# A one-block vision transformer on one core: ternary weights turned through low bf16 halves, score bias by row groups, warm-up from a constant tensor, value factors and scale row apart

## What is computed

```python
h = patches @ W.T + b + pos_emb                       # 512 x 256
z = layernorm(h)
k, q, v = split(z @ W_kqv + b_kqv)                    # 16 heads of 16
a = softmax(q @ k.T / 4 + slopes * tril(j - i), causal)
h = h + (a @ v) @ W_proj + b_proj
z = layernorm(h)

def bitlinear(x, w):
    scale = clip(mean(abs(w), axis=1), 1e-5)
    tern = clip(round(w / scale), -1, 1)
    return x @ (tern * scale).T
r = relu(bitlinear(z, w_fc) + gate * (z @ v.T @ fast_b.T @ u.T))   # 1024 hidden
out = h + bitlinear(r * r, w_proj)
```

## Time and profile before

| | before |
|---|---|
| median of 3 runs | 71.55 us (71.11 to 71.77) |
| the profiled execution | 70.84 us |
| its span in the trace | 69.0 us |
| PE busy in the span | 61.9 us (90%) |
| weight loads (PEld) | 55.6 us (80%) |
| DVE, ACT, POOL busy | 45.6, 38.4, 25.9 us |
| read from and written to memory | 6.08 and 0.52 MB |

### The profile page before, as it was taken

How to read it: one execution, slowest core, us unless ns; L and a number is a source line. 1 busy time by engine, 2 the same in 40 slices (tenths; PEclk the granted TensorE clock), 3 DMA queues, 4 the chain that set the end, 5 groups by cost and what they waited for, 6 DMA issues and landing times.

```text
span 69.0 us, 2144 instructions
## 1 busy us (share of the span) xinstructions
PE 61.9 (90%) x886; PEld 55.6 (80%) x886; DVE 45.6 (66%) x99; ACT 38.4 (56%) x76; POOL 25.9 (37%) x41
## 2 busy tenths in 40 slices
PE   3999999999989999999999967999976999999900
PEld 2787888889979999897988836989936899999900
DVE  1000029567999877997999783426596999969670
ACT  5200001824395969947779996737949338964000
POOL 6400408597779389999915000000000000000610
PEclk9999999999999999999999999999999999999997
DMA  0899999999810000000000000000000000000053
GB/s 0 269 310 312 321 385 410 419 362 369 311 64 0 9 0 0 0 9 0 9 0 0 9 5 5 0 0 9 0 0 0 0 0 0 0 0 0 9 176 128
DMA packets 3497, 6.74 MB, mean 98 GB/s; under 512 B 400, under 2 KB 1312, under 8 KB 3488
## 3 DMA queue, kind: packets, MB, share of 16 engines
q1 hardware_dynamic: 3488, 6.60, 26.5%
HBM read 6.08 MB, written 0.52 MB: 96 GB/s over the span
## 4 chain that ended last, share of the span: by engine, by line
PE 69%; DVE 12%; ACT 12%; issue 3%
PE psum L304 13%; PE psum L489 11%; PE psum L460 8%; PE psum L370 5%; PE psum L499 5%; PE psum L324 4%; PE psum L344 4%; PE psum L427 3%; PE psum L399 2%; DVE z L779 2%; PE psum L388 2%; PE psum L469 2%; ACT L696 2%; ACT fc_t L614 2%; PE psum L437 2%
## 5 line engine op out<-in xcount | busy, mean ns | idle before, releaser
L1043 POOL TENSOR_TENSOR tail_sb<-tail_sb,h 128x256 f32<-128x256 f32 x2 | 1.4, 732 | 26.3 <-DVE tail_sb L878 26.3
L719 ACT ACTIVATE head_sb<-psum,fc_scale 128x256 f32<-128x256 f32 x16 | 6.7, 470 | 4.6 <-PE psum L469 3.7
L593 ACT ACTIVATE std<-mv,eps_sb 128x1 f32<-128x1 f32 x8 | 2.2, 288 | 12.5 <-DVE mv L773 12.5
L489 PE MATMUL psum<-mlp_t,sq_hi 128*128 128x256 f32 x32 | 7.9, 285 | 1.1 <-DVE sq_lo L797 1.0
L489 PE MATMUL psum<-mlp_t,sq_lo 128*128 128x256 f32 x32 | 7.7, 281 | 0.0
L769 DVE TENSOR_TENSOR h<-psum,pos_sb 128x256 f32<-128x256 f32 x4 | 1.6, 412 | 8.9 <-PE psum L304 8.9
L489 PEld LDWEIGHTS psum<-mlp_t,sq_hi 128*128 128x128 f32 x32 | 6.0, 189 | 1.5 <-issue 1.5
L460 PE MATMUL psum<-zt_hi,fc_t 128*128 128x256 f32 x32 | 6.7, 281 | 0.0
L304 PE MATMUL psum<-head_sb 128*128 128x256 f32 x24 | 6.7, 445 | 0.0
L460 PE MATMUL psum<-zt_lo,fc_t 128*128 128x256 f32 x32 | 6.6, 278 | 0.0
L304 PEld LDWEIGHTS psum<-head_sb 128*128 128x128 f32 x24 | 5.5, 235 | 1.0
(11 more groups left out here) (111 smaller groups left out, 164.7 us busy)
## 6 DMA issues: line engine op xcount, KB each, us to landing
head_sb<-head SPq DMA_DIRECT2D x6, 256.0 KB, 4.2
fc_sb<-w_fc SPq DMA_DIRECT2D x2, 512.0 KB, 7.0
mlp_sb<-w_mlp SPq DMA_DIRECT2D x2, 512.0 KB, 8.9
tail_sb<-tail SPq DMA_DIRECT2D x2, 384.0 KB, 6.1
out<-tail_sb SPq DMA_DIRECT2D x4, 128.0 KB, 1.7
pos_sb<-pos SPq DMA_DIRECT2D x1, 256.0 KB, 4.6
kqv_sb<-w_k SPq DMA_DIRECT2D x1, 256.0 KB, 6.5
kqv_sb<-w_q SPq DMA_DIRECT2D x1, 256.0 KB, 6.7
```

The lines of the kernel that those rows point to most:

```text
L489: mm = pe.matmul(mlp_ps[f * BH + b], part[:, n % RING, a, b * P:(b + 1) * P], mlp_t[:, 2 * j + a, :], start=j == 0 and a == 0 and i == 0 a ...
L719: nc.scalar.activation(relu[:, n % PART_RING, a, :], FCB[n][:, a * HT:(a + 1) * HT], ACT.Relu, scale=fc_scale[:, 0, m:m + 1]).then_inc(rel ...
```

## The change

Four things are edited.

1. **Turning the ternary weights.** `ROUND` gets 2^14 added. The low 16 bits of the rounded float32 are then 0x4000 plus the whole number, and read as bf16 that is 2.0 for zero, a little more for a positive and a little less for a negative number. `fc_low` and `mlp_low` are views of these low halves (bf16, every second one). PE turns them as ordinary bf16 matmuls against `ident_bf`, and ACT subtracts 2 instead of `ROUND` before the sign. POOL has to make `ident_bf` from `ident`.
2. **Score bias.** The table has 128 columns instead of 256. Partitions 0 to 63 hold the heads of the first score bank, 64 to 127 those of the second; inside each 64, 32 rows are the high part and 32 the low part. `score_bias` is two matmuls with 64 rows each, against `select_r`, that adds a high and a low row. POOL makes `select_r` and subtracts twice on 32 partitions. The constants carry 8 columns more.
3. **Warm-up.** The 14 matmuls read a constant tensor of ones that exists before the program's first barrier, so `warm`, its memset on DVE and PE's wait for it go.
4. **Side products apart.** `fold_v` stays where `fold_v_spread_scale` was, without its wait for `mlp_scaled`. `spread_scale` stands behind `turn(0)` of the second layernorm, ahead of `turn_mlp(1)`. ACT's copy is 32 columns at the old place (`vf_sb`), and 256 columns (`scale_row`) behind `mlp_signs(1)`.

The core of the diff:

```diff
-ROUND = 1.5 * 2.0 ** 23
+ROUND = 1.5 * 2.0 ** 23 + 2.0 ** 14
...
-        warm = sb("warm", [P, HT], BF16)
+        ones = nc.const_aps.tensor(1.0, [P, HT], BF16)
...
+        fc_low, mlp_low = (w[:, :, :].rearrange("p m e -> p (m e)").bitcast(BF16).rearrange("p (w two) -> p w two", two=2)[
+            :, :, 0].rearrange("p (m e) -> p m e", e=n) for w, n in ((fc_whole, E), (mlp_whole, HID)))
...
             def score_bias(f):
-                pe.wait_ge(alibi_step, 4)
-                pe.wait_ge(identr_done, 1)
+                pe.wait_ge(alibi_step, 5)
+                pe.wait_ge(select_done, 1)
                 for r in range(2):
-                    for i, part in enumerate((alibi_hi, alibi_lo)):
-                        bias = part[:, r * HPG:(r + 1) * HPG, :].rearrange("p (o h) s -> p o (h s)", o=1)
-                        pe.matmul(s_ps[f][:, r, :], ident_r[:, :], bias.broadcast_to([P, BH, HPG * S]),
-                                  start=i == 0, stop=False, skip_group_check=True)
+                    rows = slice(r * 64, (r + 1) * 64)
+                    bias = bias_t[rows, :, :].rearrange("p (o h) s -> p o (h s)", o=1)
+                    pe.matmul(s_ps[f][:, r, :], select_r[rows, :, :].rearrange("p h s -> p (h s)"),
+                              bias.broadcast_to([64, BH, HPG * S]), start=True, stop=False, skip_group_check=True)
...
-            def fold_v_spread_scale():
+            def fold_v():
                 pe.wait_ge(v0_in, 16)
+                for k in range(KE):
+                    mm = pe.matmul(vf_ps[:, k * RANK:(k + 1) * RANK], v_sb[:, k * P:(k + 1) * P], v_sb[:, E:E + RANK],
+                                   start=True, stop=True)
+                mm.then_inc(vf_done, 1)
+
+            def spread_scale():
                 pe.wait_ge(mlp_scaled, 1)
...
             def turn_fc(i):
+                pe.wait_ge(ident_half, 1)
...
-                        mm = pe.transpose(fct_ps[i][:, k, m * P:(m + 1) * P], fc_whole[:, 4 * i + m, k * P:(k + 1) * P],
-                                          ident)
+                        mm = pe.matmul(fct_ps[i][:, k, m * P:(m + 1) * P], fc_low[:, 4 * i + m, k * P:(k + 1) * P],
+                                       ident_bf[:, :], start=True, stop=True)
...
-                        mm = pe.transpose(mlpt_ps[i][:, m // 2, c:c + P], mlp_whole[:, o, h], ident)
+                        mm = pe.matmul(mlpt_ps[i][:, m // 2, c:c + P], mlp_low[:, o, h], ident_bf[:, :],
+                                       start=True, stop=True)
...
-            pe.wait_ge(warm_set, 1)
             for _ in range(WARM_PRODUCTS):
-                pe.matmul(bank[7][:, 0:HT], warm[:, 0:P], warm[:, :], start=True, stop=True)
+                pe.matmul(bank[7][:, 0:HT], ones[:, 0:P], ones, start=True, stop=True)
...
-            fold_v_spread_scale()
+            fold_v()
             project(0)
-            pe.wait_ge(side_copied, 1)
+            pe.wait_ge(vf_copied, 1)
             turn_mlp(0)
...
             turn(0, z, z2t_ps[0], z2_ready, z2t_turned)
+            spread_scale()
             pe.wait_ge(duo_ready, 6)
             turn_mlp(1)
...
             mlp_signs(1)
+            copy_out(scale_row[:, :], row_ps, row_done, 1, row_copied)
...
-            dve.memset(warm[:, :], 0.0).then_inc(warm_set, 1)
             dve.memset(eps_sb[:, :], EPS).then_inc(eps_set, 1)
```

More of the change, by code:

```diff
@@ L49 @@
 C_SLOPE = C_IMG + 2
-C_GATE = C_SLOPE + H
+C_SEL = C_SLOPE + HPG
+C_GATE = C_SEL + S
 C_QB = C_GATE + 1
@@ L79, in build_program @@
         v_sb = sb("v_sb", [RANK, E + RANK])
-        side_sb = sb("side_sb", [P, KE * RANK + E])
-        vf_sb = side_sb[:, 0:KE * RANK].rearrange("p (k r) -> p k r", r=RANK)
-        scale_row = side_sb[:, KE * RANK:KE * RANK + E]
+        vf_sb = sb("vf_sb", [P, KE, RANK])
+        scale_row = sb("scale_row", [P, E])
         ident = const_sb[:, C_ID:C_ID + P]
@@ L619, in mlp_signs @@
                 nc.scalar.activation(mlp_t[:, 4 * i:4 * i + 4, :].rearrange("p (a b) e -> p a (b e)", a=2), mlpt_ps[i],
-                                     ACT.Sign, bias=minus_round[:, 0:1]).then_inc(mlpt_ready, 1)
+                                     ACT.Sign, bias=minus_two[:, 0:1]).then_inc(mlpt_ready, 1)
             def query_copy(f):
```

73 lines of the change are left out of this document (39 added, 34 removed).

## The result

The changed kernel takes 71.79 us (median of 20 executions, 71.05 to 73.2), the kernel before 71.24 us beside it (20 executions, 70.26 to 71.77). The ratio is 1.011, with a 95% interval from 1.0077 to 1.0144: it is about 1% slower, where I forecast 0.8% faster. The ratios here leave out executions more than 1.5% above the fastest of the same kernel; the medians of all twenty give 1.008.

The account below looks back on a forecast made before the run. PE was taken to bound the chain at its start and from 42.14 us on, with DVE and ACT between. Terms 0.15 + 0.05 + 0.32 = 0.52 us off the 71.55 us median gave 71.0 us, range 70.3 to 72.0.

Parts of the forecast that it names:

- Start, 0.15 us: Start of PE's stream: without the wait for the memset, work starts sooner; 0.15 us won, bounds 0 and 0.2.
- two caps: Limits on PE's 0.25 us sooner start: embedding records at the lower clock, and block 2's transfer landing at 10.1 us.
- ACT at the second `std`, 0.05 us: Second layernorm: ACT is 0.5 to 0.6 us sooner, but DVE is late next; 0.05 us won, bounds 0 and 0.1.
- Turn, 0.32 us: Eight mlp turns ahead of `hidden_main`: step 0.065 instead of 0.105 us; 0.32 us won, bounds 0 and 0.41.
- Score bias, 0: Scores on PE: two matmuls fewer per half, DVE 0.15 us sooner but then standing longer behind POOL; nothing counted.
- The knot of DVE and POOL: DVE's L842 at 33.87 us takes 1.37 instead of 0.74 us, seemingly standing behind POOL's 1024-wide rounding.
- Moved pieces, 0.02 us and hidden: `spread_scale` behind `turn(0)`: PE's idle hides all but 0.02 us; ACT's copy is hidden with 0.1 us to spare.
- Nothing arrives: Rival, chance 0.18: strided turns cost as float32, transfer or clock takes the start's gain; 0.0 to 0.1 won, 71.5 us.
- The knot opens: Rival, chance 0.20: DVE's L842 goes ahead of POOL's rounding, up to 0.63 us back; with 0.4 left, 70.6 us.
- Unhidden pieces: Rival, chance 0.10: `spread_scale` starts only after `turn(0)` drains, or the scale copy meets `low_high`; 0.3 us each, 71.9 us.
- The clock: Rival, chance 0.10: the clock rises later in the embedding; six more slow records give +0.75 us, seven or eight 72.4.
- my sign of about seven: Embedding on PE: the forecast is wrong if the number of records at the long step is not about seven.

Follow-up runs that it names:

- The control on DVE: Sixteen one-column memsets added on DVE to the changed kernel, nothing on PE; 72.17 us, ratio to before 1.0129.
- the two matmuls more: Two matmuls of 4 columns, result unread, added behind `fold_v` in the changed kernel; 70.35 us timed, ratio to before 0.9908.
- 8 matmuls more: Eight matmuls of 4 columns, result unread, added behind `fold_v` in the changed kernel; 70.29 us, ratio to before 0.9904.
- turns doubled: The changed kernel with the eight turns of `turn_fc(1)` done twice; 70.26 us, ratio to before 0.9884.
- idle filled: The changed kernel with `turn_fc(1)`'s eight turns done twice and eight 128-column matmuls behind `fold_v`; 70.28 us, ratio to before 0.9887.
- old bias: The changed kernel with the score bias of the kernel before; 70.43 us, ratio to before 0.9893.
- four matmuls: Four matmuls of 4 columns, result unread, added behind `fold_v` in the changed kernel; 71.35 us in one execution.
- the bias alone: The kernel before with only the new score bias; 71.38 us, ratio to before 1.0028.
- with the scales at the new and at the old place: Old place: the changed kernel with `turn_fc(1)`'s turns done twice, `spread_scale` and its copy back beside `fold_v`; 70.5 us, ratio to before 0.9947.
- turns alone: The kernel before with only the bf16 turns of the ternary weights; 71.98 us, median of four executions.
- warm-up alone: The kernel before with only the new warm-up (constant ones, no memset or wait); 70.91 us, ratio to before 0.9938.
- seven and twelve warm-ups: The changed kernel with 7 warm-up matmuls of 512 columns, or 12 with two of 512, instead of 14; 71.25 us and 72.77 us.

## Why the prediction was wrong

**The sum and the step that failed.** For the computation 0.52 us was forecast and 0.55 is seen at the last add. That it came out so well is luck in part: of the three terms one gave nothing (0 for 0.15) and one far more than I took (0.24 for 0.05), and they cancel; and two traces of one kernel can lie 0.4 us apart. The step that failed is the last of the working, that from `hidden_main` to the end PE's chain has the same instructions as before and moves along. The chain did; the end didn't. The step went from the end of the computation to the end of the program as if the outputs cost the same, and they cost 1.2 us more (3.7 instead of 2.6 us from the last add to the end). The control on DVE, the two matmuls more and the table show this to be the fetch of PE's instructions. With a short tail the changed kernel takes 70.3 to 70.4 us in the five timed kernels built on it (8 and 2 matmuls more, turns doubled, idle filled, old bias), so without the late fetch the edit gains about 1%.

**Start, 0.15 us: 0.** I named two caps, and the first was another: the last `head_sb` piece lands at 9.08 and PE now waits 0.38 us for it. PE's stretch without a gap in the earlier trace rows I took as a sign that the pieces were early; it only said that none was late yet. Block 2 starts where it did, so the lower bound, 0, was the value in this pair of traces. In the other traces it starts anywhere from 10.11 to 10.67 us with the new warm-up and from 10.45 to 10.62 with the old one, as the transfers land, so one pair can't settle a term of 0.15.

**ACT at the second `std`, 0.05 us: 0.24.** It starts at 40.07 instead of 40.31. I held DVE to be late next, at 40.26, and had not read that DVE stood 0.33 us in "issue" just ahead of that block. This idle time is gone with the memset of the warm-up, in every trace, and then ACT's 0.5 us of reserve, which the forecast had as the value without DVE's lateness, came through in part. The new place of the scales is needed for it: without it ACT is 0.44 us late.

**Turn, 0.32 us: 0.26.** The step from one turn to the next is 0.068 us (eight from 37.80 to 38.34), close to the forecast 0.065, and the eight take 0.58 us to `hidden_main` with the change of operand. The Trainium skill's 81 ns for such a pair (TensorE: Matmul & The Clock Gate, Back-to-back issue gap) is too long for this stream by these rows. Eight steps are 0.54 us, and the change to `hidden_main`'s operand takes the rest, which I had not counted. The stride of two costs nothing that these rows show.

**Score bias, 0: 0.** The reason was wrong. The knot of DVE and POOL did stay as it was (33.89 and 1.35 us; the earlier trace rows have 33.87 and 1.37), but the bias never brought DVE 0.15 us sooner: PE's `scores(0)` starts at 21.91 instead of 21.88 us and `scores(1)` at 28.11 instead of 28.08. Before `scores(0)` PE's weight load had stood 0.15 us in "issue", at 20.0 us; before `scores(1)` PE now waits 0.18 us for ACT's `q_pad`. With the one switch more that the prediction named, this gives back what the two matmuls less save.

**Moved pieces, 0.02 us and hidden: as said.** PE went on without idle from L418 to L445; ACT's copy fitted with 0.19 us to spare instead of 0.1.

**The rivals.** Nothing arrives: refuted, 0.55 us arrived at the last add. The knot opens: refuted by its row. Unhidden pieces: refuted. The clock: more slow embedding records did not come, the trace has fewer (the long steps end at 4.9 instead of 6.6 us), so my sign of about seven was off, on the harmless side. But in 6 of 20 executions the mean clock was below 0.98. None of these has a trace; in the traces of two kernels built on the changed one (old bias, four matmuls) it fell to half at 36 to 37 us, behind PE's idle time in the middle. The faster turns lengthen that idle time: PE waits 0.69 us ahead of `fold_v` in after and not at all in before. A PE that finishes sooner and waits is what I should have priced. The result fell within the range, 70.3 to 72.0, and on the slower side; there I had only the clock and the unhidden pieces, and it was neither. The share of the forecast that I counted under 70.83 us, four tenths, was also too high: 0.13 of the 0.6 us from 70.7 to 71.3 lie there.

## What to carry over

Look at the instruction queue of the profile as at any other transfer: where it lies relative to the last outputs, and whether a dense run of small matmuls stands behind one of its packets. A few instructions more or less on PE can cost or give 1.2 us in this 71 us kernel without touching any work, so a small edit should be timed with two or three layouts of its stream (two idle matmuls were enough here) before it is thrown away. And read the start of an engine's last "issue" idle and the next input's landing before a gain upstream is carried through to the end.

## What the runs showed of the hardware

- TensorE's stream (882 matmuls and 882 weight loads in the trace of after) comes in packets of 16 KB during the run, each 0.9 to 1.7 us long on one DMA engine (q8 has seven in the whole of after). What places the last one is open, and the count alone doesn't: from the changed kernel's 1.47 us behind the first output, 4, 8 and 16 instructions more all put it 0.93 to 0.95 ahead, and 32 put it 8.3 ahead; the bias alone, also with 882 matmuls, has it 5.35 behind; and of two kernels with 890 (turns doubled, with the scales at the new and at the old place) one has it 0.94 and the other 0.35 ahead.
- In five traces an output issue (SyncE) that was under way while such a packet moved took 0.57 to 1.81 us instead of 0.33 or 0.34, and ended 0.31 to 0.38 us behind the packet. It was never the first of the four: where the first began inside the packet (before, turns alone) it kept its 0.35 us.
- 256 instructions of small products in 1.8 us can outrun the fetch: PE stood 0.13 to 1.04 us in `scores(0)` in five kernels (warm-up alone, 8 matmuls more, bias alone, seven and twelve warm-ups).
- The granted clock fell to half for 3 to 4 us behind PE's idle time in some executions of a kernel and not in others (three traces have such a fall). What decides it is open: 1.03 of 2 us busy and a fall with four small matmuls, 1.14 busy and none with two.
- DVE's 0.33 us of "issue" idle at 39 us went with one memset at the program's start. Why is open.
